# Second attention's query sum moved to GpSimd, final phase in tiles of 128 flat tokens, and two GpSimd subtractions split by channel half, in a two-layer cross-attention and expert kernel

## What is computed

```
x = x + attention0(layernorm(x), ctx)   # 16 heads: softmax(q k' / 4) v
x = x + experts0(layernorm(x))          # each token goes to 1 of 8 experts
x = x + attention1(layernorm(x), ctx)   # 8 heads: o = q + softmax(q k' / 16) v
                                        # o = LN(o)*g0+b0; o += relu(o Wo + bo); o = LN(o)*g1+b1
x = x + experts1(layernorm(x))          # the best 2 of 8 gated experts per token,
                                        # g = a*sigmoid(b), then one shared down projection Wo
```

## Time and profile before

| What | Value |
|---|---|
| median of 3 runs | 1878.34 us |
| the profiled execution | 1879.33 us |
| its span (first to last instruction) | 1877.2 us |
| mean granted TensorE clock | 0.905 of 2.4 GHz |
| PE / PE weight load busy | 85% / 64% |
| VectorE / ScalarE / GpSimd busy | 57% / 43% / 43% |
| attention(0), routing(0) and expert_tiles | about 0 to 860 us |
| attention(1) | about 860 to 1486 us |
| routing(1) | 1487 to 1538 us |
| gated tiles / last phase | 1539 to 1760 / 1760 to 1877 us |

### The profile page before, as it was taken

One profiled execution on the slowest core, in us unless ns is written; L12 is line 12 of the kernel. 1 busy time (PEld: TensorE's weight loads), 2 busy tenths in 40 slices (PEclk: granted clock), 3 DMA queues, 4 the chain that ended last, 5 costly groups with the idle time before them and its releaser, 6 DMA issues. The chain is left out here.

```text
span 1877.2 us, 48532 instructions
## 1 busy us (share of the span) xinstructions
PE 1602.5 (85%) x16482; PEld 1195.6 (64%) x16483; DVE 1070.6 (57%) x2269; ACT 806.9 (43%) x1574; POOL 816.0 (43%) x1127
## 2 busy tenths in 40 slices
PE   5999999999944999995999999999998329999667
PEld 4777777777732666664777777777777314444345
DVE  3666666666634222222677766776667466766445
ACT  3777777777730222222655455545555101111111
POOL 3666666666631111113555454545554113333363
PEclk8999999999976999997998888988889559999879
DMA  4112121111014111112112111211110203333464
GB/s 123 53 55 75 53 75 53 30 30 30 16 45 182 33 32 34 34 31 82 32 59 73 55 51 55 73 33 29 32 29 11 100 27 103 105 108 109 116 162 115
DMA packets 57879, 119.23 MB, mean 64 GB/s; under 512 B 12556, under 2 KB 30964, under 8 KB 54484
## 3 DMA queue, kind: packets, MB, share of 16 engines
q1 hardware_dynamic: 45348, 90.25, 14.7%
q0 software_dynamic: 12464, 28.08, 5.6%
HBM read 89.32 MB, written 28.97 MB: 63 GB/s over the span
## 5 line engine op out<-in xcount | busy, mean ns | idle before, releaser
L968 DVE TENSOR_REDUCE a_mx<-a_SM 100x2 bf16<-100x722 f32 x384 | 351.5, 915 | 198.7 <-PE a_SM L431 192.0
L706 ACT ACTIVATE a_Pr<-a_ST 120x1600 f32<-120x1600 f32 (+3 forms) x192 | 225.3, 1173 | 160.6 <-PE a_ST L463 159.8
L755 POOL TENSOR_TENSOR a_rstd<-a_ve,a_powers 100x1 f32<-100x1 f32 x192 | 114.3, 595 | 325.3 <-DVE a_ve L938 324.3
L431 PE MATMUL a_SM<-a_KT,a_QM 32*100 32x362 f32 x768 | 159.8, 412 | 60.3 <-DVE a_mx L968 55.7
L1705 PE MATMUL g_PH<-w,g_xT 128*128 x456 | 207.1, 597 | 0.0
L473 PE MATMUL a_M<-a_Pr,a_V 120*32 120x100 f32 (+3 forms) x4608 | 198.7, 270 | 0.0
L473 PEld LDWEIGHTS a_M<-a_Pr,a_V 120*32 120x32 f32 (+3 forms) x4608 | 155.0, 130 | 24.1 <-issue 14.3
L431 PEld LDWEIGHTS a_SM<-a_KT,a_QM 32*100 32x100 f32 x768 | 64.6, 164 | 120.8 <-DVE a_mx L968 92.2
L1705 PEld LDWEIGHTS g_PH<-w,g_xT 128*128 128x128 f32 x456 | 83.1, 192 | 83.6 <-issue 83.6
L361 PE MATMUL a_M<-a_ch,a_wkh 128*128 128x362 f32 x256 | 100.7, 393 | 29.1 <-POOL a_cl L823 28.7
L812 POOL TENSOR_TENSOR a_KL<-a_KF,a_KT 128x724 fp32r<-128x724 f32 x64 | 111.1, 1737 | 30.8 <-ACT a_KT L599 30.7
(11 more groups left out here) (198 smaller groups left out, 3714.0 us busy)
## 6 DMA issues: line engine op xcount, KB each, us to landing
w<-in_E_w SPq DMA_DIRECT2D x24, 1024.0 KB, 6.0
a_ct<-in_ctx SPq DMA_DIRECT2D x64, 362.0 KB, 3.1
gated_rows<-g_hs SPq DMA_DIRECT2D x57, 256.0 KB
keep_rows<-a_keep SPq DMA_DIRECT2D x64, 100.0 KB
tile_rows<-e_y SPq DMA_DIRECT2D x32, 128.0 KB, 1.7
b_rows<-in_E_b SPq DMA_DIRECT2D x1, 4096.0 KB
out<-g_y SPq DMA_DIRECT2D x32, 100.0 KB
X<-in_x SPq DMA_DIRECT2D x1, 2800.0 KB
```

Of the source, the lines that this page charges most:

```text
L431: last = nc.tensor.matmul(SM[0:LQ, half, 0:LKP], QM[b.p][rows, chunk, m, :], KT[b.p][rows, chunk, :], start=True, stop=True)
L706: nc.scalar.activation(Pr[0:n, s, :].rearrange("p (r q) -> p r q", r=GROUPS), ST[0:n, :, 0:PER * LQ], ACT.Exp, scale=SCALE).then_inc(exp_d ...
L755: nc.gpsimd.tensor_tensor(rstd[k][:], ve[k][:].to_broadcast([LQ, n]), powers[:, 0:n], ALU.pow).then_inc(rstd_ready[k], 1)
L968: V_.tensor_reduce(pair, SM[0:LQ, :, 0:LK], AX_X, ALU.max).then_inc(max_done, 1)
```

## The change

Three edits. First, in layer 1 of `attention`, the addition of the projected query to the attention's output (line 1002) goes from VectorE to GpSimd, at the end of GpSimd's step; `tail1c` comes right after `tail1a` on VectorE; and GpSimd's order in a step changes, with one new wait ahead of `low_context` and the index copy of a gather (`gather_rows`) parted from the gather. Second, in both layers the subtractions of `low_parts` and `low_context` are issued as two instructions, one for each half of the channels (128x362 each). Third, the last phase runs over 25 tiles of 128 tokens in flat order (partition p holds tokens 25p to 25p+24) with a ring of 4 buffers. For that, attention(1) also stores X of each sequence to DRAM (`x_rows`), routing(1) loads it back flat and turns slots and weights to flat order by four transposes, an eviction, a store and a load, and `gated_tiles` reads them so.

```diff
 # attention, SP
+                if layer == 1:
+                    sp.wait_ge(x3_ready, b.count(1, 1))
+                    sp.dma_start(t["x_rows"][bass.ds(b.at * LQ, LQ), :],
+                                 X[0:LQ, bass.ds(b.at, 1), :].rearrange("q o d -> q (o d)")).then_inc(x_stored, 16)
...
+            if layer == 1:
+                sp.wait_ge(x_stored, 16 * NB)
 # attention, GpSimd
+            def queries_added(b):
+                pool.wait_ge(norm_read, b.count(1, 1))
+                pool.wait_ge(qtok_biased, b.count(1, 1))
+                nc.gpsimd.tensor_tensor(o[:], o[:], qtok[b.p][:], ALU.add).then_inc(qtok_used, 1)
...
-                nc.gpsimd.tensor_tensor(KL[b.p][:], KF[:], KT[b.p][:], ALU.subtract).then_inc(kl_ready, 1)
+                for c in range(DC):
+                    last = nc.gpsimd.tensor_tensor(KL[b.p][:, c, :], KF[:, c, :], KT[b.p][:, c, :], ALU.subtract)
+                last.then_inc(kl_ready, 1)
...
-                nc.gpsimd.tensor_tensor(cl[b.p][:], ct[b.p][:], ch[b.p][:], ALU.subtract).then_inc(cl_ready, 1)
+                for c in range(DC):
+                    last = nc.gpsimd.tensor_tensor(cl[b.p][:, c, :], ct[b.p][:, c, :], ch[b.p][:, c, :], ALU.subtract)
+                last.then_inc(cl_ready, 1)
 # GpSimd's step
+                if tail and layer == 1:
+                    power(1, prev)
                 if fr:
                     low_parts(nxt)
-                if tail and layer == 1:
-                    power(1, prev)
                 if ahead and layer == 1:
+                    if tail:
+                        pool.wait_ge(o1_ready, prev.count(1, 1))
                     low_context(nxt2)
+                if ends:
+                    residual1(prev2)
                 if ahead:
                     power(0, nxt2)
-                if ends:
-                    residual1(prev2)
...
+                if ahead and layer == 1 and nxt2.low + 1 < NB:
+                    gather_rows(nxt2.plus(1))
+                if fr:
+                    masked_low(nxt)
                 if ends:
                     power(3, prev2)
-                if fr:
-                    masked_low(nxt)
...
                 if ahead and layer == 1 and nxt2.low + 1 < NB:
                     gather(nxt2.plus(1))
+                if back and layer == 1:
+                    queries_added(b)
 # attention, VectorE
-                dve.wait_ge(qtok_biased, b.count(1, 1))
-                V_.tensor_tensor(o[:], o[:], qtok[b.p][:], ALU.add).then_inc(qtok_used, 1)
                 dve.wait_ge(qtok_used, b.count(1, 1))
...
                     if tail and j == 0:
                         tail1a(prev)
-                    if tail and j == 1:
                         tail1c(prev)
 # routing, layer 1: SP, ScalarE, TensorE, VectorE (one more constant, ident, is loaded first)
+                sp.dma_start(env["X"][:, 0:FLAT, :], t["x_rows"].rearrange("(p i) d -> p i d", i=FLAT)
+                             ).then_inc(flat_loaded, 16)
+                sp.wait_ge(by_seq_ready, 1)
+                sp.dma_start(t["lists"].rearrange("k b q -> b k q"), by_seq[:]).then_inc(by_seq_stored, 16)
+                sp.wait_ge(by_seq_stored, 16)
+                sp.dma_start(env["flat"][:], t["lists"].rearrange("k b q -> k (b q)").rearrange(
+                    "k (p i) -> p k i", i=FLAT)).then_inc(flat_loaded, 16)
+                sp.wait_ge(flat_loaded, 32)
...
+                act.wait_ge(flat_ps, 1)
+                nc.scalar.activation(by_seq[:].rearrange("b k q -> b (k q)"), PS[0:NB, 3, 0:4 * LQ], ACT.Copy
+                                     ).then_inc(by_seq_ready, 1)
...
                 pe.wait_ge(slots_ready, k + 1)
+                if k == 1:
+                    pe.wait_ge(flat_ready, 4)
+                    for a in range(4):
+                        last = nc.tensor.transpose(PS[0:NB, 3, a * LQ:(a + 1) * LQ], by_token[:, a, :],
+                                                   ident[0:LQ, 0:LQ])
+                    last.then_inc(flat_ps, 1)
...
+                if layer == 1:
+                    V_.tensor_copy(by_token[:, k, :], den[:]).then_inc(flat_ready, 1)
+                    dve.wait_ge(flat_ready, 3 + k)
 # gated_tiles (FLAT = TOK // 128 = 25)
-    RING = 8
+    RING = 4
-        GR = [sb(f"GR{p}", [LQ, 2, GH]) for p in range(RING)]
+        GR = [sb(f"GR{p}", [128, 2, GH]) for p in range(RING)]
...
-            for b in range(NB):
+            for b in range(FLAT):
                 sp.wait_ge(y_ready, b + 1)
-                sp.dma_start(t["out_rows"][b * LQ:(b + 1) * LQ, :], y[b % DEEP][:]).then_inc(y_stored[b % DEEP], 16)
+                sp.dma_start(t["out_rows"].rearrange("(p i) d -> p i d", i=FLAT)[:, b, :], y[b % DEEP][:]
+                             ).then_inc(y_stored[b % DEEP], 16)
...
-                                                 bass.IndirectOffsetOnAxis(env["slots"][k][:, b:b + 1], 0)
+                                                 bass.IndirectOffsetOnAxis(where[:, k, b:b + 1], 0)
...
-                    last = nc.tensor.transpose(PT[:, g * LQ:(g + 1) * LQ], comb[b % 2][:, g * 128:(g + 1) * 128],
-                                               ident[0:LQ, 0:LQ])
+                    last = nc.tensor.transpose(PT[:, g * 128:(g + 1) * 128], comb[b % 2][:, g * 128:(g + 1) * 128],
+                                               ident[:])
```

More of the change, by code:

```diff
@@ L36 @@
 TOK = NB * LQ
+FLAT = TOK // 128
 LN_EPS = 1e-5
@@ L887, in step @@
                     gather(nxt2.plus(1))
+                if back and layer == 1:
+                    queries_added(b)
             if layer == 1:
-                gather(fixed(0))
-                gather(fixed(1))
+                for b in range(2):
+                    gather_rows(fixed(b))
+                    gather(fixed(b))
             nc.gpsimd.memset(powers[:, 0:1], -0.5)
@@ L1684, in _ @@
             pool.wait_ge(g_stored[1], 16 * (NT // 2))
-            for b in range(NB):
+            pool.wait_ge(where_ready, 1)
+            for b in range(FLAT):
                 pair_of_rows(b)
@@ L1743, in _ @@
             turn(0)
-            for b in range(NB):
-                if b + 1 < NB:
+            for b in range(FLAT):
+                if b + 1 < FLAT:
                     turn(b + 1)
@@ L1814, in _ @@
                 tile(j, j, 0, j, False, j)
-            with dve.Fori(1, NB // 2) as i:
+            with dve.Fori(1, FLAT // 2) as i:
                 for p in range(2):
                     tile(i * 2 + p, p, i, 2, False, i * 2 + p)
-            with dve.Fori(NB // 2, (NT - 2) // 2) as i:
+            for j in range(FLAT // 2 * 2, FLAT // 2 * 2 + 2):
+                tile(j, j % 2, j // 2, 2, False, j if j < FLAT else None)
+            with dve.Fori(FLAT // 2 + 1, (NT - 2) // 2) as i:
                 for p in range(2):
```

84 lines of the change are left out of this document (50 added, 34 removed).

## The result

The changed kernel took 1765.85 us (median of 4 runs, 1764.86 to 1772.18) against 1877.82 (4 runs, 1876.98 to 1880.26) for the kernel before on the same chip: a ratio of 0.9409, 95% interval 0.9385 to 0.9433. Its span is 1764.2 us against 1877.2, its mean granted clock 0.936 against 0.905.

What follows compares the result with a forecast made beforehand. Attention(1) was taken to be bound by VectorE–GpSimd collisions that idle TensorE and lower its clock. Terms -62 - 2 + 0.5 + 0.5 + 3.5 - 17 = -76.5 gave 1802 us, range 1779 to 1838 (8 in 10).

Steps and rivals of the forecast that it cites:

- the loop of attention(1): 24 steps of attention(1): from a mean of 18.78 us to 16.2, a gain of 62 us, bounds 43 and 74.
- peeled steps: Attention(1)'s steps outside the loop, which have no slow member: a gain of 2 us, bounds 0 to 4.
- the last phase: 25 periods of 2.17 us gain 12 us, fewer stalls 5: together 17 us faster, bounds 8 and 27.
- the late X sum: Attention(1): X sum ahead of power(0) ends VectorE's 1.62 us wait; fast steps lose TensorE's 0.73 us idle gap, reaching 16.3.
- The lower bound: Attention(1)'s loop: steps no shorter than 15.7 us, TensorE's busy time in the fast step.
- rival C: Attention(1): one parity keeps a 2 us block, now at line 1010; mean step 18.35 us, total 1855; chance 0.08.
- Halves: Low-part subtractions in both layers: no gain, 0.5 us of cost in the two first steps, bounds -3 and +4.
- The stores of X: Attention(1): 32 more DMAs on SP, only the last landing before the barrier; +0.5 us, 0 to 2.
- Routing(1): Turning slots and weights to flat order at the end of routing(1): net +3.5 us, bounds 0 and 7.
- A: Attention(1): steps stop at 17.0 us, collisions moving to line 1013 or 950; total 1823 us; chance 0.2.
- B: Last phase does not shorten, its stalls set by the same 13 MB and a halved ring; 1819 us; chance 0.1.
- D: Attention(1): moved sum comes late for the statistics, every step costs 20.5 us; total 1907 us, slower; chance 0.04.

Runs made afterwards that it cites:

- the added wait: Kernel before, with one wait added: GpSimd's key subtraction starts only when VectorE's sum with the queries is done; X sum in its old place; 1844.09 us.
- the exchange: Kernel before, with only GpSimd's X sum put ahead of power(0); 1791.07 us, ratio 0.9535.

## Why the prediction was wrong

Of the 36 us, 22 are the loop of attention(1), 5 its peeled steps and 9 the last phase.

**Attention(1)'s loop: the step that failed.** I let steps of 20.5 us become such of 17.0, took 0.73 us off both kinds for the late X sum, and bounded the result by 15.7. The gain was 24 x (18.78 - 15.27) = 84 us, where I had 62 with an upper bound of 74. The part for the collision was right in size: with the collision alone gone (the added wait), the steps took 17.0 and 17.2 us. The mis-sized term is the 0.73.

- *The late X sum was priced by TensorE's last idle gap, 0.73 us.* The runs show it worth 1.33 us (16.60 against 15.27, changed kernel) to 1.74 (17.11 with the added wait against 15.37 with the exchange). Over 24 steps that is 14 to 24 us more than I had. The wait of 1.62 us on VectorE, which stood in the same rows, was the nearer figure. The lateness was spread. With the added wait TensorE waits (lines as in the kernel before) 8.9 us before L439 and 13.4 before L431 over 20 steps, where the exchange leaves 7.0 us at L431 (21 steps) and none at L439. And a third of it counts as busy: in the two eight-step rows a step has 1.65 against 0.46 us of idle time, and 15.45 against 14.84 of busy time.
- *The peeled steps had the same lateness.* In the kernel before, the second and third step take 16.83 and 16.81 us with a sum of 0.42, so without collision, and with the exchange 15.14 and 15.20. I had 2 us for all peeled steps, at most 4; they gave 7.
- *The lower bound was no bound.* 15.7 us of "busy" TensorE includes such hidden waits; in the changed kernel the same step is busy for 14.7 to 14.8. And the window of 17.0 us held 206 matmul records, where the two windows of the changed kernel hold 201.

How long a fast step was depends on the line that one measures from. GpSimd's starts gave me 17.0, VectorE's reciprocals give 17.1, but TensorE's L439 gives 16.16. In the kernel before (timeline of PE), the two ahead of the one at 1139.45:

```profile
1102.00 0.26 PE L439 MATMUL a_ST<-a_neg_ident,a_mxr 100*128 100x100 bf16 x2 [0.72 <-DVE a_mxr L978]
...
1123.29 0.26 PE L439 MATMUL a_ST<-a_neg_ident,a_mxr 100*128 100x100 bf16 x2
```

By these the pair splits into 21.29 and 16.16 us, and 16.16 - 0.73 = 15.4 is nearly the measured 15.27. That is a match found afterwards and no run shows it to be the reason; the run with the added wait speaks for 17.0 and a larger wait.

**What made the slow parity.** I named the right lines (the sum under the key subtraction), but not what set them against each other. With the late X sum, ScalarE's copy ended 2.98 us behind VectorE's reciprocal in a slow step; with the exchange it ends 3.49 behind it. Those 0.5 us decide whether the subtraction is ready before the sum starts. So one exchange takes away both: 1.67 us of collision (18.78 - 17.11) and 1.74 of order (17.11 - 15.37). I gave the exchange 0.73 a step and the moved sum all the rest; alone, they are worth 89 and 14 us. The moved sum alone won little more than rival C's 10 us. With the new wait and the rest of the order it did end the slow parity without the exchange (1807.26), so the case as a whole did not hang on the exchange, but its size did.

**Halves.** No gain, as said, and for the reason said: two back to back hold VectorE as one does. The Trainium skill (SBUF — State Buffer, "Who interferes with whom") has the block end when the instruction holding it finishes; here it spanned the two halves (2.6 us against 0.96 for one half) and began before the recorded start of the first. The cost was 2.9 us in attention(0) where I had 0.5, within my bound of 4: I priced only the two first steps, and one parity of all steps pays 0.2.

**The last phase** gained 26.3 us, where I had 17 and at most 27. The period was right: 2.17 us, -12. The stalls gave 14, not 5. I had weighed "by the number of instructions" (8) against "by data" (none); the experiments speak for the stream of indirect DMAs. With 25 gathers there are no stalls, with 50 the phase stands 25 us above those 65.7, and the 64 of before cost 39 (116.7 less 32 x 2.07 + 11). The change cut the gathers and the ring at once. With a ring of 4 in both kernels the stalls cost 35 and 25 us, with a ring of 8 in both 39 and at most 34. So the two share the gain; one profile of each does not part them further. The Trainium skill (Runtime: NRT & Kernel Launch, "Instruction fetch mechanics") was no help: the phase in loops stalls alike, and the unrolled one with half the gathers does not stall.

**Small terms.** The stores of X show nowhere, within my 2 us. Routing(1) and the end of attention(1): +1.5 together, for +0.5 and +3.5; the store and the load of the lists pass beside the matmuls of L1278 and VectorE's last lines, instead of ahead of them.

**Rivals.** A's steps of 17.0 are those of the kernel before with the added wait; the change did not meet them, because the X sum went first. B did not come about. C's block did, in the kernel with the moved sum alone. D did not come about: VectorE's statistics waited 0.64 us behind line 1032, ahead of 1.55 us of room.

**Open.** No row shows what passes between TensorE's end and the start of ScalarE and VectorE in the last phase, and so how a dense stream of indirect DMAs delays them. Unrolled code, waiting for stores and bytes are excluded by a run each; the mechanism is not found.

## What to carry to other kernels

When steps alternate with the same work, look for a small wait that shifts one engine's phase before blaming the collision that it ends in; here reordering two short instructions was worth six times moving the blocked one. The last idle gap of TensorE (0.73 us) is not the price of a wait that recurs in every step: here the whole wait (1.62 us) came nearer to the 1.33 to 1.74 measured. Do not take TensorE's busy time as a lower bound for a step, and measure steps over pairs, from lines of several engines. Where GpSimd gathers in a dense stream, look at the number and spacing of the gathers, not at their bytes.

## What the hardware showed unexpectedly

- A GpSimd instruction of two SBUF inputs that is ready, but by its recorded start still queued behind a 0.58 us power instruction, goes with a VectorE two-input sum that is held: 2.42 to 2.61 us in all of 20 steps where its operand was ready 0.20 us or more before the sum's start, 0.42 to 0.44 in all of 70 where it was not. With a semaphore wait ahead of it (start 0.2 us later) the sum was not held in any of 7 such steps.
- With 50 indirect DMAs issued 1.25 us apart, ScalarE and VectorE stood for 32.0 to 45.8 us (five profiles) in waits of up to 7.3 us that the profile puts down as remote. With 25 of them, at a median of 2.25 us, there was no such wait, at 145 GB/s. With 50 and a pause of 0.59 us at each tile it was 2.3 and 25.5 us. Halving the bytes left 44.3 us.
